# A fused Mamba and mixture-of-experts layer on one core: the load of C's row moves behind a slot's other loads, and the scaling of b2 moves four slots later

## The chip, the core and the metric

The kernel runs on one core of a Trainium2 chip. Time is the device time of one execution in microseconds (us), the median of several runs. The profile shows five engines: PE (TensorE), DVE (VectorE), ACT (ScalarE), POOL (GpSimd) and SP (SyncE, which here issues nearly all loads and stores and computes nothing). Each engine works through its own program in order and waits on semaphores for the others.

## The reference, cut to what matters

The input x is 4 x 2048 tokens of 512 features. The layer does two things to it.

```
mod = silu(c) @ wmod                       # six rows of 512 per batch: sa, ca, ga, sb, cb, gb
h = layernorm(x) * (1 + ca) + sa
x = x + ga * mamba(h)                      # ga, gb kept at least 0.25 from zero
h = layernorm(x) * (1 + cb) + sb
x = x + gb * moe(h)

mamba(h):  val, gate = split(h @ W_in);  val = silu(conv3(val))
           B, C = val @ W_B, val @ W_C;  delta = softplus((val @ W_delta + delta_base) @ W_tau)
           A_bar = exp(delta*A);  B_bar = expm1(delta*A)/(delta*A + 1e-6) * delta * B
           for each of 512 channels and 16 states:  s_t = A_bar_t * s_(t-1) + B_bar_t * val_t
           y_t = sum over the 16 states of s_t * C_t;  out = (y * silu(gate)) @ W_out + h
moe(h):    gates = top 2 of sigmoid(h @ gate_W), normalised
           sum over 8 experts of gate_e * (gelu(h @ W1_e + b1_e) @ W2_e + b2_e), plus one shared expert
```

## The kernel before, in words

The tokens are cut into 16 blocks of 512 (NQ). The recurrence is done in *units* of 128 channels by 1024 columns, 32 units in all. A unit has 16 states, and one state of one unit is one *slot* of the program: 512 slots, numbered c, behind 64 slots of lead-in (c below 0) and before 64 slots of tail. 32 slots make a *window*, r = c mod 32. In each slot every engine does its part of the recurrence for a state and, beside it, the steps of two other jobs that a table assigns to r: the *front* of a later block (normalise, the projections val, gate, B, C, delta, the convolution, all stored to DRAM) and the *FFN* of an earlier block (out projection, gating, the experts). PACE says how many steps of front and FFN go with a slot: one in the steady part, about 1.6 in slots 0 to 48, 1.5 in slots 448 to 512.

The recurrence of a slot goes over the engines like this:

- ACT makes `inv`, `th` and `abar` for four states at a time.
- PE broadcasts B's row to 128 partitions (L1162).
- DVE multiplies by u (L1179), by abar+1 (L1185), by the weight `inv` (L1191), by the ratio (L1198), and scans (L1209) into `hs`. These five are DVE's main work.
- POOL, in slot c: the product `hs * Cb` of state c-1 (`times_C`, L1363 or L1366), then steps of the FFN or front (newton L1397 to L1403, gating of the hidden rows L1452, and the split of B), then the weight `inv * th` of state c+2 (L1390), then it issues the accumulating DMA that adds `hs` of state c-1 to `ysum` (`add_to_y`, L1374 or L1377). That DMA waits until the one before it has landed (`y_summed`), because both add to the same tile. In this text y(c) is the transfer that adds state c's product.

`Cb` holds C's row of one state, broadcast to 128 partitions, in two buffers. SP loads the row of state c+1 in slot c (L680, 512 KB), after waiting for `hC_done >= c`, which is the product of state c-1, the last reader of that buffer. In the kernel before, this wait and load come first in SP's slot, and everything else that SP issues in the slot stands behind them:

```
for t in SLOTS:
    sync_slot(sp, t)                  # wait hC_done >= t; load Cb; then delta, us, Brow, gy and gated_y
    for H, r in steps_of(t):
        sync_steps(sp, H, r)          # loads and stores of the front and the FFN
    sync_slot_end(sp, t)              # the folding of ga and gb into W_out, W2 and b2
```

Many of the steps in `sync_steps` have waits of their own: a weight buffer (`aw`, `w1r`, `w2r`) is loaded when the matmuls that read it are done, a store waits for its producer. The steps named later: at r = 11 the loads of `gy` (L711) and of three `aw` (L535); at r = 13 the store of `gate_rows` (L567); at r = 23 a load of `w1r` (L544), a row of `gbc` (L564) and three `w2r` (L556); at r = 27 a load of `gy`; at r = 28 the loads of W_out into `w1r` (L654, 1 MB) and of the residual into `hf` (L656, 1 MB).

In slots -8 to 40 the kernel also folds ga and gb into the weights, one batch (12 slots) after another: SP loads a piece, POOL multiplies it (L1429), SP stores it. For b2 it is DVE that multiplies (L1217), into a piece of `w2r`, and SP stores the result (L739) at the end of slot 12b+5 for batch b. DVE may write the next batch's only when that store has landed (`fold_b2st`). In the kernel before DVE does this at the head of slots 12b-6, that is -6, 6, 18 and 30, each time (but the first) one slot behind the issue of the store it waits for.

Of the kernel before, what the change touches and what calls it, by code (L numbers as in the profile page):

```python
# [24 lines left out]
def adaln_mamba_moe(nc, x, W_val, W_gate, taps, W_BC, W_deltaT, delta_base, W_tau, A_log, W_out, gate_W, W1, b1, W2, b2,  # L25
# [7 lines left out]
    NB, L, D = x.shape  # L33
# [16 lines left out]
    WIN = 2 * N  # L50
# [27 lines left out]
    with ExitStack() as ctx:  # L78
# [8 lines left out]
        def ge(eng, s, value):  # L87
            if value > 0:
                eng.wait_ge(s, value)
# [329 lines left out]
        NF = 6  # L419
# [18 lines left out]
        def unit(c):  # L438
            return c // N
# [13 lines left out]
        def starts(u):  # L453
            return 0 <= u < NU and u in FIRST_U

        def fronts(u):
            q, n = BLOCKS[BLOCK_OF[u]]
            return q + n
# [209 lines left out]
            ge(sp, abar_done, N * (u - 1))  # L668
            sp.dma_start(tile_of(delta[:, u % 2, :], u), rows_of(delta_d, u)).then_inc(u_ld[u % 2], 16)

        def sync_slot(sp, c):
            r = c % WIN
            if 0 <= c + 1 < NC:
                u, n = unit(c + 1), (c + 1) % N
                q, size = BLOCKS[BLOCK_OF[u]]
                ge(sp, hC_done, c)
                if n == 0 and starts(u):
                    sp.wait_ge(st_c, 16 * fronts(u))
                row = c_d[q // 2, n, :] if size == 2 else c_d[q // 2, n, columns(q)]
                sp.dma_start(Cb[:, (c + 1) % 2, 0:size * T], row.partition_broadcast(P)).then_inc(C_ld[(c + 1) % 2], 16)  # L680
            if r in (1, 17) and 0 <= c // N + 1 < NU and not starts(c // N + 1):
                load_unit(sp, c // N + 1)
            if r in (8, 24) and 0 <= c // N + 1 < NU:
                u = c // N + 1
                if starts(u):
                    sp.wait_ge(st_u, 16 * fronts(u))
                ge(sp, uB_done, N * (u - 1))
                sp.dma_start(tile_of(us[:, u % 2, :], u), rows_of(u_d, u)).then_inc(us_ld[u % 2], 16)
            if r == 24 and starts(c // N + 1):
                k = BLOCK_OF[c // N + 1]  # L690
                q, n = BLOCKS[k]
                sp.wait_ge(st_b, 16 * (q + n))
                row = b_d[q // 2] if n == 2 else b_d[q // 2, :, :, columns(q)]
                if k > 1:
                    sp.wait_ge(B_ready, N * FIRST_U[k - 1])
                lo = BROW * (k % 2)
                sp.dma_start(Brow[lo:lo + 3 * N, 0:n * T], row.rearrange("j n t -> (j n) t")).then_inc(B_ld[k % 2], 16)
            if r in (2, 18) and 0 <= c // N - 1 < NU:
                u = c // N - 1
                sp.wait_ge(y_gated, u + 1)  # L700
                sp.dma_start(rows_of(gy_d, u), tile_of(gy[:], u)).then_inc(gy_st, 16)

            if r in (11, 27) and 0 <= c // N < NU:
                u = c // N
                ge(sp, gy_st, 16 * u)
                if u + 1 < NU:
                    sp.wait_ge(nr_minus, u + 2)
                    sp.wait_ge(nrd_done, u + 2)
                if starts(u):
                    sp.wait_ge(st_gate, 16 * fronts(u))  # L710
                sp.dma_start(tile_of(gy[:], u), rows_of(gate_d, u)).then_inc(gate_ld, 16)  # L711
# [456 lines left out]
        def dve_slot(dve, c):  # L1168
            v = nc.vector

            def X(c):
                return flat(ps[:, X_BANK + 2 * (c % 2):X_BANK + 2 * (c % 2) + 2, :])

            def times_u(c):
                if 0 <= c < NC:
                    u = unit(c)
                    dve.wait_ge(B_ready, c + 1)
                    dve.wait_ge(us_ld[u % 2], 16 * (u // 2 + 1))
                    v.scalar_tensor_tensor(X(c), X(c), 1.0, us[:, u % 2, :], ALU.mult, ALU.mult).then_inc(uB_done, 1)  # L1179

            def times_abar(c):
                if 0 <= c < NC:
                    dve.wait_ge(abar_done, c + 1)
                    dve.wait_ge(uB_done, c + 1)
                    v.scalar_tensor_tensor(X(c), abar[:, c % 4, :], 1.0, X(c), ALU.add, ALU.mult).then_inc(p1_done, 1)  # L1185

            def times_weight(c):
                if 0 <= c < NC:
                    dve.wait_ge(thinv_done, c + 1)
                    dve.wait_ge(p1_done, c + 1)  # L1190
                    v.scalar_tensor_tensor(X(c), X(c), 1.0, inv[:, c % 6, :], ALU.mult, ALU.mult).then_inc(pw_done, 1)  # L1191

            def times_ratio(c):
                if 0 <= c < NC:
                    u = unit(c)
                    dve.wait_ge(pw_done, c + 1)
                    for cols, g in parts(u):
                        ins = v.scalar_tensor_tensor(X(c)[:, cols], nrd[:, u % 2, cols], inv_kappa[:, c % N, g:g + 1],  # L1198
                                                     X(c)[:, cols], ALU.add, ALU.mult)
                    ins.then_inc(bu_done, 1)  # L1200

            def scan(c):
                if 0 <= c < NC:
                    u = unit(c)
                    dve.wait_ge(bu_done, c + 1)
                    if c >= 4:
                        dve.wait_ge(y_summed, 16 * (c - 3))
                    for cols, g in parts(u):
                        ins = v.tensor_tensor_scan(hs[:, c % 4, cols], abar[:, c % 4, cols], X(c)[:, cols],  # L1209
                                                   0.0 if begins(u) else carry[:, g, c % N:c % N + 1], ALU.mult, ALU.add)  # L1210
                    ins.then_inc(scan_done, 1)

            if 0 <= c + 6 < 2 * NF * NB and (c + 6) % (2 * NF) == 0:
                b = (c + 6) // (2 * NF)
                dve.wait_ge(fold_rows, 32 * (b + 1))
                ge(dve, fold_b2st, 16 * b)
                v.tensor_tensor(fold_b2g, b2g, gbc[BROW:BROW + EX, 1, :], ALU.mult).then_inc(fold_b2, 1)  # L1217
            times_weight(c)
            for H, r in steps_of(c)[:1]:
                dve_steps(dve, H, r, True)  # L1220
            times_ratio(c)
            times_u(c + 1)
            scan(c)
            times_abar(c + 1)
            for i, (H, r) in enumerate(steps_of(c)):
                if i:
                    dve_steps(dve, H, r, True)
                dve_steps(dve, H, r)
# [253 lines left out]
        with nc.Block() as block:  # L1482
            @block.sync
            def _(sp):
                for t in SLOTS:
                    sync_slot(sp, t)
                    for H, r in steps_of(t):
                        sync_steps(sp, H, r)
                    sync_slot_end(sp, t)
                for tt in range(TPB):  # L1490
                    sp.wait_ge(out_st[tt], 16 * NQ)
# [73 lines left out]
```

## Time and profile before

| | |
|---|---|
| median of 3 runs | 4697.77 us (4693.6 to 4699.59) |
| the profiled execution's own time | 4694.18 us |
| its span, first to last instruction | 4692.4 us |
| DVE busy | 4033.8 us (86%) |
| ACT busy | 3945.9 us (84%) |
| PE busy | 3849.1 us (82%) |
| POOL busy | 3647.7 us (78%) |
| granted TensorE clock, mean | 0.888 of full speed |
| moved by DMA | 1037.18 MB, mean 221 GB/s |

"Busy" is the sum of an engine's instruction times. No engine is at 100%, and the stretch matters: from 225 us to 774 us (slots 0 to 63) there is no FFN, from 774 us to 3860 us (slots 64 to 447) all three jobs run side by side, then the FFN is squeezed into fewer slots, and behind 4484 us (slot 511's scan) only the last FFN remains. A wait is listed under the engine that idled, with the line of the instruction it idled before, and behind the arrow what ended the wait.

### The profile page before, as it was taken

The numbers are of one execution on the slowest core, as the hardware profiler recorded it, in microseconds if no ns is written. First come the engines' busy times: TensorE is split into PE (matmuls) and PEld (weight loads), VectorE is DVE, ScalarE is ACT, GpSimd is POOL, SyncE is SP. The second block draws the span as 40 slices with busy tenths as digits, with TensorE's granted clock in tenths as the row PEclk, the third lists the DMA queues.
The fourth block names the chain that finished last, engine by engine and source line by source line (L and its number), as shares of the span: only waits on it lengthen the run. The fifth ranks groups of instructions, "written<-read, shape, count | busy, mean of one in ns | idle before, by whom it ended". The sixth has DMA issues, their size and how long they took to land.

```text
span 4692.4 us, 37024 instructions
## 1 busy us (share of the span) xinstructions
PE 3849.1 (82%) x9708; PEld 1612.3 (34%) x9708; DVE 4033.8 (86%) x3896; ACT 3945.9 (84%) x4282; POOL 3647.7 (78%) x2304
## 2 busy tenths in 40 slices
PE   6623413999899899989998998999998987988889
PEld 3201101333343333333343333333333333333344
DVE  1288899999999999999999999999999997887820
ACT  1698898998989898999989898989999897887811
POOL 0399987887889888888889888888888896767721
PEclk7856656999999999999999999999999988989889
DMA  3589867888888888888888888898988876657542
GB/s 131 197 247 266 236 170 198 238 235 255 231 253 233 257 246 258 232 251 248 242 255 234 254 235 258 236 267 221 264 252 236 238 210 166 192 154 196 138 146 67
DMA packets 352220, 1037.18 MB, mean 221 GB/s; under 512 B 41253, under 2 KB 44389, under 8 KB 344710
## 3 DMA queue, kind: packets, MB, share of 16 engines
q1 hardware_dynamic: 278282, 766.35, 47.9%
q0 software_dynamic: 73728, 268.47, 29.0%
q8 instruction: 78, 1.28, 0.1%
q14 instruction: 132, 1.08, 0.1%
HBM read 639.74 MB, written 126.51 MB: 163 GB/s over the span
## 4 chain that ended last, share of the span: by engine, by line
ACT 21%; PE 19%; DMA 13%; POOL 13%; issue 13%; DVE 8%; POOLq 0%; SPq 0%; DVEq 0%; ACTq 0%
DMA ysum<-hs 13%; PE ps L1125 7%; PE ps L1144 6%; POOL inv L1390 4%; POOL hs L1363 3%; ACT inv L761 3%; ACT th L772 3%; PE ps L1095 3%; ACT inv L767 3%; ACT abar L776 2%; ACT inv L754 2%; DVE ps L1191 2%; DVE ps L1179 2%; POOL ysum L1377 2%; DVE ps L1185 2%
## 5 line engine op out<-in xcount | busy, mean ns | idle before, releaser
L1390 POOL TENSOR_TENSOR inv<-inv,th 128x1024 f32<-128x1024 f32 x512 | 1268.0, 2477 | 148.8 <-ACT th L772 146.5
L1125 PE MATMUL ps<-hf,w1r 128*128 128x512 f32 x2304 | 1104.0, 632 | 38.6 <-ACT hid L884 23.3
L1363 POOL TENSOR_TENSOR hs<-hs,Cb 128x1024 f32<-128x1024 f32 x384 | 977.3, 2545 | 30.1 <-DVE hs L1209 13.2
L1162 PE MATMUL ps<-Brow,pick 48*128 48x512 bf16 x1024 | 346.6, 422 | 630.2 <-DVE hs L1209 629.1
L1144 PE MATMUL ps<-w2r,hid 128*128 128x512 f32 x1776 | 812.1, 604 | 0.8 <-ACT xn L884 0.7
L754 ACT ACTIVATE inv<-nrd,kappa 128x1024 f32<-128x1024 f32 (+1 forms) x640 | 578.6, 967 | 201.5 <-DVE ps L1191 197.4
L1179 DVE SCALAR_TENSOR_TENSOR ps<-ps,us 128x1024 f32<-128x1024 f32 x512 | 628.0, 1227 | 134.0 <-PE ps L1162 133.5
L1377 POOL DMA_DIRECT2D ysum<-hs x480 | 442.6, 922 | 367.4 <-DMA ysum<-hs 356.9
L1191 DVE SCALAR_TENSOR_TENSOR ps<-ps,inv 128x1024 f32<-128x1024 f32 x512 | 627.9, 1226 | 81.0 <-POOL inv L1390 59.2
L1198 DVE SCALAR_TENSOR_TENSOR ps<-nrd,inv_kappa,ps 128x1024 f32<-128x1024 f32 (+1 forms) x640 | 675.2, 1073 | 15.8
L1209 DVE TENSOR_TENSOR_SCAN hs<-abar,carry,ps 128x512 f32<-128x512 f32 (+1 forms) x384 | 683.5, 1801 | 0.3
L776 ACT ACTIVATE abar<-delta,negA 128x1024 f32<-128x1024 f32 (+1 forms) x640 | 605.6, 965 | 78.0 <-DVE hs L1209 78.0
L1125 PEld LDWEIGHTS ps<-hf,w1r 128*128 128x128 f32 x2304 | 448.7, 201 | 612.5 <-issue 562.9
L1185 DVE SCALAR_TENSOR_TENSOR ps<-abar,ps 128x1024 f32<-128x1024 f32 x512 | 618.2, 1207 | 0.1
L772 ACT ACTIVATE th<-delta,halfA 128x1024 f32<-128x1024 f32 (+1 forms) x640 | 605.2, 965 | 5.8 <-POOL inv L1390 5.8
L767 ACT ACTIVATE inv<-inv,ln_coef 128x1024 f32<-128x1024 f32 (+1 forms) x640 | 607.0, 967 | 1.5
L1209 DVE TENSOR_TENSOR_SCAN hs<-abar,ps 128x1024 f32<-128x1024 f32 (+1 forms) x256 | 511.6, 2009 | 0.3
L1144 PEld LDWEIGHTS ps<-w2r,hid 128*128 128x128 f32 x1776 | 332.1, 192 | 450.4 <-issue 447.5
L761 ACT ACTIVATE inv<-inv 128x2048 f32<-128x2048 f32 x256 | 478.9, 1902 | 1.3
L1162 PEld LDWEIGHTS ps<-Brow,pick 48*128 48x128 bf16 x1024 | 58.6, 97 | 991.1 <-DVE hs L1209 788.9
L1366 POOL TENSOR_TENSOR hs<-hs,Cb 128x1024 f32<-128x1024 f32 x128 | 311.7, 2435 | 35.6 <-DVE hs L1209 27.6
L1248 DVE TENSOR_TENSOR x<-ps,x 128x512 f32<-128x512 f32 x256 | 171.9, 682 | 170.4 <-PE ps L1144 147.6
(154 smaller groups left out, 5021.2 us busy)
## 6 DMA issues: line engine op xcount, KB each, us to landing
ysum<-hs POOLq DMA_DIRECT2D x512, 512.0 KB, 5.7
Cb<-c_rows SPq DMA_DIRECT2D x384, 512.0 KB, 4.6
w1r<-in_W SPq DMA_DIRECT2D x144, 512.0 KB, 5.3
w2r<-w_scaled SPq DMA_DIRECT2D x141, 512.0 KB, 8.1
Cb<-c_rows SPq DMA_DIRECT2D x128, 256.0 KB, 4.0
gbc<-expert_gates SPq DMA_DIRECT2D x128, 256.0 KB, 5.4
aw<-in_W_val SPq DMA_DIRECT2D x64, 256.0 KB, 6.3
xa<-in_x SPq DMA_DIRECT2D x32, 512.0 KB, 7.2
```

The source lines that it names most:

```text
L767: ins = s.activation(inv[:, c % 6, cols], inv[:, c % 6, cols], ACT.Exp, scale=-1.0, bias=ln_coef[:, c % N, g:g + 1])
L772: ins = s.activation(th[:, c % 3, cols], delta[:, u % 2, cols], ACT.Tanh, scale=halfA[:, c % N, g:g + 1])
L776: ins = s.activation(abar[:, c % 4, cols], delta[:, u % 2, cols], ACT.Exp, scale=negA[:, c % N, g:g + 1])
L1125: mm = t.matmul(o, w1r[:, n % 2, k, h * P:(h + 1) * P], hf[:, k, :], start=(k == 0), stop=(k == G - 1))
L1144: mm = t.matmul(o, hidden(e)[:, h, tt * P:(tt + 1) * P], (last_w2(e) if q == NQ - 1 and grp == 1 else w2r[:, e % 3])[:, h, :], start=(grp ...
L1179: v.scalar_tensor_tensor(X(c), X(c), 1.0, us[:, u % 2, :], ALU.mult, ALU.mult).then_inc(uB_done, 1)
L1185: v.scalar_tensor_tensor(X(c), abar[:, c % 4, :], 1.0, X(c), ALU.add, ALU.mult).then_inc(p1_done, 1)
L1191: v.scalar_tensor_tensor(X(c), X(c), 1.0, inv[:, c % 6, :], ALU.mult, ALU.mult).then_inc(pw_done, 1)
L1198: ins = v.scalar_tensor_tensor(X(c)[:, cols], nrd[:, u % 2, cols], inv_kappa[:, c % N, g:g + 1], X(c)[:, cols], ALU.add, ALU.mult)
L1209: ins = v.tensor_tensor_scan(hs[:, c % 4, cols], abar[:, c % 4, cols], X(c)[:, cols], 0.0 if begins(u) else carry[:, g, c % N:c % N + 1], ...
L1363: gp_.tensor_tensor(hs[:, c % 4, :], hs[:, c % 4, :], Cb[:, c % 2, :], ALU.mult).then_inc(hC_done, 1)
L1390: gp_.tensor_tensor(inv[:, c % 6, :], inv[:, c % 6, :], th[:, c % 3, :], ALU.mult).then_inc(thinv_done, 1)
```

## The change

SP's load of C's row is taken out of the head of `sync_slot` into a function `load_C` of its own, which is called after the front's and FFN's steps of the slot and before `sync_slot_end`. Its wait (`hC_done >= c`) goes with it. So what stood behind that wait in slot t now stands behind the wait of slot t-1 only, and the load of C's row stands behind whatever waits the slot's other steps have. DVE's scaling of b2 goes from slots 12b-6 to slots 12b-2 (-2, 10, 22, 34).

```
-        def sync_slot(sp, c):
-            r = c % WIN
+        def load_C(sp, c):
             if 0 <= c + 1 < NC:
                 u, n = unit(c + 1), (c + 1) % N
                 q, size = BLOCKS[BLOCK_OF[u]]
                 ...
                 row = c_d[q // 2, n, :] if size == 2 else c_d[q // 2, n, columns(q)]
                 sp.dma_start(Cb[:, (c + 1) % 2, 0:size * T], row.partition_broadcast(P)).then_inc(C_ld[(c + 1) % 2], 16)
+
+        def sync_slot(sp, c):
+            r = c % WIN
             if r in (1, 17) and 0 <= c // N + 1 < NU and not starts(c // N + 1):
...
-            if 0 <= c + 6 < 2 * NF * NB and (c + 6) % (2 * NF) == 0:
-                b = (c + 6) // (2 * NF)
+            if 0 <= c + 2 < 2 * NF * NB and (c + 2) % (2 * NF) == 0:
+                b = (c + 2) // (2 * NF)
                 dve.wait_ge(fold_rows, 32 * (b + 1))
                 ge(dve, fold_b2st, 16 * b)
...
                     for H, r in steps_of(t):
                         sync_steps(sp, H, r)
+                    load_C(sp, t)
                     sync_slot_end(sp, t)
```

## Rows read from the trace of the kernel before

**Rows 1.** The page's chain that ended last: shares of the span by line.
```profile
DMA ysum<-hs 13%; PE ps L1125 7%; PE ps L1144 6%; POOL inv L1390 4%; POOL hs L1363 3%; ACT inv L761 3%; ACT th L772 3%; PE ps L1095 3%; ACT inv L767 3%; ACT abar L776 2%; ACT inv L754 2%; DVE ps L1191 2%; DVE ps L1179 2%; POOL ysum L1377 2%; DVE ps L1185 2%
```

**Rows 2.** By stage: stretch, length, busy us PE, PEld, DVE, ACT, POOL; clock, DMA, GB/s.
```profile
225.00:656.00 431.00, 153.61 (x337) 52.85 (x338) 373.89 (x391) 373.19 (x515) 389.36 (x254) 0.63 0.82 239
774.00:3860.00 3086.00, 2783.76 (x7059) 1153.90 (x7057) 2974.82 (x2679) 2850.18 (x2799) 2648.88 (x1663) 0.94 0.85 244
```

**Rows 3.** Waits of DVE, 774 to 3860 us: total us, times, longest.
```profile
DVE ps L1191 <- POOL inv L1390: 54.1, 34, 3.6
```

**Rows 4.** Waits of POOL, 774 to 3860 us.
```profile
POOL ysum L1377 <- DMA ysum<-hs: 315.0, 120, 6.1
```

**Rows 5.** Waits, 3860 to 4484 us: DVE's largest.
```profile
DVE ps L1179 <- PE ps L1162: 102.5, 31, 7.6
```

**Rows 6.** Waits of DVE, 225 to 656 us.
```profile
DVE w2r L1217 <- DMA b_scaled<-w2r: 37.7, 3, 14.0
DVE ps L1191 <- POOL inv L1390: 4.4, 2, 3.2
```

**Rows 7.** POOL in time order behind DVE's three stalls: start, us, what, [idle <- releaser].
```profile
283.11 0.19 POOL L1359 COPY carry<-hs 128x2 f32<-128x2 f32 x1 [1.27 <-DVE hs L1209]
393.20 0.19 POOL L1359 COPY carry<-hs 128x2 f32<-128x2 f32 x1 [2.46 <-DVE hs L1209]
504.53 0.19 POOL L1359 COPY carry<-hs 128x2 f32<-128x2 f32 x1 [1.35 <-DVE hs L1209]
```

**Rows 8.** SP in order of time, r = 27 and 28 of one window.
```profile
2028.13 0.32 SPq L711 DMA_DIRECT2D gy<-gate_rows  x1
2033.99 0.48 SPq L654 DMA_DIRECT2D w1r<-w_out_scaled  x1
2034.52 0.52 SPq L656 DMA_DIRECT2D hf<-h_residual  x1
```

**Rows 9.** POOL in order of time there: y(26), y(27), y(28) are issued.
```profile
2029.48 1.73 POOL L1377 DMA_DIRECT2D ysum<-hs  x1
2035.75 1.00 POOL L1377 DMA_DIRECT2D ysum<-hs  x1
2047.31 0.88 POOL L1377 DMA_DIRECT2D ysum<-hs  x1 [3.55 <-DMA ysum<-hs]
```

**Rows 10.** The chain of waits in order of time: start, us, what.
```profile
1004.25 11.90 DMA ysum<-hs
...
2035.75 11.02 DMA ysum<-hs
...
3833.32 10.68 DMA ysum<-hs
```

**Rows 11.** SP, then POOL, in order of time around r = 11 of the next window.
```profile
2144.01 9.37 SPq L680 DMA_DIRECT2D Cb<-c_rows  x2
2153.49 0.39 SPq L711 DMA_DIRECT2D gy<-gate_rows  x1
2153.92 1.46 SPq L535 DMA_DIRECT2D aw<-in_W_val  x3
2168.25 0.46 SPq L567 DMA_DIRECT2D gate_rows<-xa  x1
...
2164.59 0.87 POOL L1377 DMA_DIRECT2D ysum<-hs  x1 [3.74 <-DMA ysum<-hs]
```

**Rows 12.** SP in order of time, r = 22 to 24, then POOL's product of state r = 24.
```profile
1992.73 0.32 SPq L680 DMA_DIRECT2D Cb<-c_rows  x1
1997.58 1.39 SPq L556 DMA_DIRECT2D w2r<-w_scaled  x3
...
2008.66 2.65 POOL L1363 TENSOR_TENSOR hs<-hs,Cb 128x1024 f32<-128x1024 f32 x1
```

**Rows 13.** The page's DMA issues (tile, KB each, median us to landing); below it Cb's spread.
```profile
ysum<-hs POOLq DMA_DIRECT2D x512, 512.0 KB, 5.7
...
DMA to landing us min/median/max: 3.0/4.5/12.9
```

More of the change, by code:

```diff
@@ L669, in load_unit, with load_C @@
             sp.dma_start(tile_of(delta[:, u % 2, :], u), rows_of(delta_d, u)).then_inc(u_ld[u % 2], 16)
-        def sync_slot(sp, c):
-            r = c % WIN
+        def load_C(sp, c):
             if 0 <= c + 1 < NC:
@@ L680, in sync_slot @@
                 sp.dma_start(Cb[:, (c + 1) % 2, 0:size * T], row.partition_broadcast(P)).then_inc(C_ld[(c + 1) % 2], 16)
+        def sync_slot(sp, c):
+            r = c % WIN
             if r in (1, 17) and 0 <= c // N + 1 < NU and not starts(c // N + 1):
@@ L1211, in scan @@
                     ins.then_inc(scan_done, 1)
-            if 0 <= c + 6 < 2 * NF * NB and (c + 6) % (2 * NF) == 0:
-                b = (c + 6) // (2 * NF)
+            if 0 <= c + 2 < 2 * NF * NB and (c + 2) % (2 * NF) == 0:
+                b = (c + 2) // (2 * NF)
                 dve.wait_ge(fold_rows, 32 * (b + 1))
@@ L1488, in _ @@
                         sync_steps(sp, H, r)
+                    load_C(sp, t)
                     sync_slot_end(sp, t)
```

## The prediction

> **What bounds the kernel now.** I read the busy times by stage first, then each engine's waits in the long stage, then the chain of waits, and last the order of time around the places that the change touches.
>
> The long stage, slots 64 to 447, takes 3086 us or 12 windows of 257 us, and DVE is busy in 2974.8 of them, 96% [rows 2]. The reader is to see two things there: DVE sets the pace, and it is idle for only 111 us. 54.1 us of that idle is in front of L1191, waiting for POOL's weight `inv` [rows 3], so 4.5 us a window is all that a faster POOL could give back. A slower POOL has no such limit. POOL itself waits 315.0 us for the previous accumulating transfer y [rows 4], 26 us a window, and these transfers are the largest line of the chain, 13% of the span [rows 1]. So POOL with its chain of y transfers runs level with DVE and overtakes it only at a few slots. What reaches POOL is how long each y takes: the median is 5.7 us [rows 13], and y(27), issued just behind two loads of 1 MB, takes 11.02 us and makes POOL wait 3.55 us before y(28) [rows 8, 9]. Eleven such y(27), from 1004.25 to 3833.32, stand in the chain of waits [rows 10].
>
> From 3860 to 4484 us PE decides: DVE waits 102.5 us for B's broadcast, its largest wait there [rows 5]. Behind 4484 us no row of C is loaded any more, and nothing changes. From 225 to 656 us (slots 0 to 48) DVE, ACT and POOL are busy 374, 373 and 389 of 431 us [rows 2]: nearly balanced, POOL a little ahead.
>
> **b2, four slots later.** Removed: DVE's three waits for the b2 store, 37.7 us [rows 6]. The scaling itself stays. Its store was issued at the end of slot 12b+5, the new place is five slots later instead of one, so the wait is gone and not moved. What is late next is POOL. Behind each of the three stalls POOL waited for DVE's scan by 1.27, 2.46 and 1.35 us [rows 7], together 5.1 us; its remaining time was work and transfers, which do not start earlier because DVE is free. The bounds are thus 5.1 and 37.7 us gained. DVE waited for POOL's weight by only 4.4 us in the whole stretch [rows 6], so behind the last stall it can run some way ahead of POOL's lead before it is caught. I take twice POOL's share: -10 us. From 656 us to 774 us there is no folding left for POOL, and the lead is kept.
>
> **What SP issues a slot earlier.** A step without a late wait of its own used to start when the product of state c-1 was done. Now it starts one product earlier, behind the previous row of C. No engine waits much for these loads, so their being early is worth nothing in itself. What changes is which y they run beside. Bytes and issues are the same; only the collisions move.
>
> At r = 28 SP issues W_out and the residual, 2 MB, at 2033.99, 1.8 us ahead of y(27) at 2035.75 [rows 8, 9]. They have been allowed for long, so after the change they follow at once on what r = 27 ends with. That is the load of `gy`, bound by its own wait at 2028.13, then C's row, then these two: about 2028.8 and 2029.3, just ahead of y(26) at 2029.48. I give y(26) the 11.02 us that y(27) has now; with `gy` and C's row beside it that is no overestimate. POOL can then issue y(27) at 2029.48 + 11.0 + 0.5 = 2041.0, not at 2035.75. Before, POOL had 2047.31 - 3.55 - 2035.75 = 8.0 us of work from y(27) to y(28), so y(28) comes at 2049.0, not 2047.31: 1.7 us late. The weights that POOL makes on the way come up to 5 us late, and DVE meets them where it has no slack, since this is the stretch where its waits for POOL lie. I take 2.0 us a window, 12 windows: +24 us. Bounds: 0 (y(27)'s gain pays for y(26)'s loss) and 5.2 us a window (2041.0 - 2035.75 with nothing recovered), +62 us.
>
> At r = 11 it goes the other way. The loads of `gy` and three `aw` (1.25 MB) stand at 2153.5 to 2155.4, around y(10), and POOL waits 3.74 us before y(11) [rows 11]. They move to the previous C load, 2144.4, and lie in the gap between two y. So this wait nearly goes. But the store of `gate_rows` (1 MB, 2168.25) also moves up by a slot, into y(11), and takes some back. Bounds 0 and 3.74 us a window; I take 1.0, since what POOL gains here must survive to the slots where DVE waits: -12 us.
>
> **The row of C behind the other steps.** A row of 512 KB lands in 4.5 us in the middle, 12.9 us at worst [rows 13], and mostly has a slot to spare. The worst place is r = 23: the row for the product at 2008.66 was issued at 1992.73 [rows 12]. Now it stands behind the `w1r`, `gbc` and three `w2r` loads, 2.25 MB, whose last waits end about 1997.6, and goes out at 1999.0. That leaves 9.7 us, between the middle and the worst landing. Late by 0 to 3 us a window; I take 0.5, so +6 us (bounds 0 and +36). In the stage after 3860 us SP waits longer for `w1r`, but PE decides there: 0.
>
> The Trainium skill (DMA: Bandwidth & Descriptors, Queues, rings and completion order) says that on each DMA engine the descriptors of one ring are consumed in ring order. By that rule C's row can't pass the loads ahead of it; its 12.9 us at worst agrees, and the sum above is by it.
>
> **The sum.** -10 + 24 - 12 + 6 = +8 us on the profiled execution's own 4694.18 us (span 4692.4 and 1.8 around it): 4702. The median of the runs shown is 3.6 us higher, 4697.77, so the forecast for a median is 4706 us. About 0.2% or 9.4 us is what a measurement of this kernel can tell from no change, so this is no change, on its slow side. The likeliest case's own range is 4695 to 4715.
>
> **The rivals.**
>
> *Slower: the collision at y(26) is paid in full.* Place: r = 28 of each window. Price: 5.2 us a window less DVE's present wait there. With 4.5 us of wait a window for POOL in all, I leave at most 1.5 to absorb it: 3.7 x 12 = 44 us, so 4706 - 24 + 44 = 4726. It decides from the point where POOL's delay exceeds what DVE has in hand at r = 31, 0 and 1. For it: eleven of the y(27) are in the chain [rows 10], so these slots are tight. Against it: y(27) itself becomes short, and y(28)'s wait of 3.55 us goes.
>
> *Faster: the loads no longer hit a transfer that counts.* If y(26) is little hurt by loads issued a bare microsecond ahead, the term of 24 us goes, y(28)'s wait goes with it (up to 3.55 us a window, of which DVE can use what it waits for POOL there, I take 1.0, 12 us), and the slot-11 gain and b2's stay: 4706 - 24 - 12 - 6 = 4664 with C's row in time. Against it: y(27) in its 11.02 us has 2.5 MB of loads issued ahead of it within 2.1 us; y(26) will have 3 MB within 1.4 us. Half way, 4682, is more likely than the end.
> The Trainium skill (DMA: Bandwidth & Descriptors, the same section) has each DMA engine go round-robin between the queue rows that have work, a packet at a time. By that rule the accumulating transfer on POOL's row would get half of each engine whatever SP has queued, and the move would cost nothing, as in this rival; the measured 11.02 us against a median of 5.7 speaks against an equal share, so the rule does not carry the sum.
>
> *b2's stall was on the path in full.* Then its term is -37.7, not -10, and the time is 4678. For it: DVE has hardly any other idle time there, 4.4 us for POOL. Against it: POOL's 389 us of work are more than DVE's 374 [rows 2], and the POOL waits that the stalls made are small [rows 7].
>
> *The change doesn't do what it says:* the steps of r = 28 or 11 have waits that hold them where they are. Then only b2 is left, 4688 to 4693. Against it: at 2033.99 they follow C's load at once.
>
> **How the numbers follow.** No change as summed: 0.36. Slower by y(26), with or without C's rows late: 0.33. Faster, through the transfers (0.14), b2 in full (0.12), or the change half empty (0.05): 0.31. The range leaves 0.1 at each side: its low end, 4663, is the faster transfers with all of their gain or b2 and some of them together, its high end, 4738, the slower rival with C's rows 1 us late in each window (+12). Faster by over 0.2%: 0.31, within 0.36, slower 0.33.
>
> **What would show it.** In the trace after: no wait in front of L1217 in DVE's list (before 37.7), and POOL's waits for DVE in 225 to 656 us smaller by some 5 us. Slots 0 to 48 shorter by about 10 us; by over 25, b2's rival is right. In each window y(26) about 11 us long and y(27) about 5, a wait of POOL before y(27) where there was none and none before y(28); if y(26) stays near 5 us, the term of 24 us is wrong. The wait before y(11) down from 3.7 us to 2 or less. DVE's wait for POOL's weight up from 54.1 us to some 70; if it falls below 40, the balance of the collisions was misjudged. POOL products that wait for C's row at r = 24, by at most 3 us: if others do, or if they wait longer, the cost of the new order was underrated. A stage from 3860 to 4484 us that changes by more than 5 us would be a mistake of its own, since I give it nothing.

## The result

| | before | after |
|---|---|---|
| median | 4695.69 us, 4 runs | 4797.09 us, 4 runs (4793.45 to 4799.68) |
| span of the profiled execution | 4692.4 us | 4797.9 us |

The ratio is 1.0216, 95% interval [1.0201, 1.0231]: 101 us slower. I had forecast 4706, called it no change, and given a range up to 4738: the sign of the sum was right, its size wrong by far, and the outcome that I held likeliest did not come.

Busy times hardly moved (DVE 4038.5 us, before 4033.8; POOL 3646.0, before 3647.7), so no work was added: the kernel waits more. From the page of the kernel after, the chain that ended last by line, two groups of instructions (busy, mean ns | idle before, releaser), and the transfers (KB each, median us to landing):

```profile
DMA ysum<-hs 13%; PE ps L1127 9%; PE ps L1146 8%; POOL hs L1365 3%; DMA Cb<-c_rows 3%; DVE ps L1181 3%; POOL inv L1392 3%; PE ps L1097 2%; DVE ps L1187 2%; DVE ps L1193 2%; ACT inv L763 2%; DVE hs L1211 2%; ACT th L774 1%; POOL ysum L1379 1%; ACT abar L778 1%
...
L1365 POOL TENSOR_TENSOR hs<-hs,Cb 128x1024 f32<-128x1024 f32 x384 | 969.2, 2524 | 98.9 <-DMA Cb<-c_rows 65.2
...
L1193 DVE SCALAR_TENSOR_TENSOR ps<-ps,inv 128x1024 f32<-128x1024 f32 x512 | 627.7, 1226 | 194.9 <-POOL inv L1392 175.5
...
ysum<-hs POOLq DMA_DIRECT2D x512, 512.0 KB, 5.6
Cb<-c_rows SPq DMA_DIRECT2D x384, 512.0 KB, 6.0
```

The reader is to see a line in the chain that [rows 1] does not have, C's row with 3%, and a product that waits for it. The median y did not get longer (5.6 us against 5.7 in [rows 13]). The averages say nothing here; what counts is which y is long. (Lines of after stand two below those of before: L1193 is the old L1191, L1365 the old L1363, L1379 the old L1377.)

A slot's length is told here from the end of one scan to the end of the next. Slots 64 to 447 took 3081.8 us before and 3180.8 after, +98.9; the part behind them +7.7; the part before them -1.1. So nearly the whole loss stands in the twelve windows, 8.2 us in each. The waits of DVE and POOL there, after (us in total, times, longest), to be held against [rows 3, 4]:

```profile
POOL ysum L1379 <- DMA ysum<-hs: 293.3, 114, 7.1
DVE ps L1193 <- POOL inv L1392: 146.6, 62, 6.1
POOL hs L1365 <- DMA Cb<-c_rows: 65.2, 21, 8.2
...
POOL ysum L1379 <- DMA Cb<-c_rows: 29.1, 13, 4.1
POOL carry L1361 <- DMA Cb<-c_rows: 29.0, 15, 5.4
```

DVE's wait for POOL's weight rose by 92.5 us (54.1 to 146.6), which is the loss but for 6 us. Waits for C's row are new. The 65.2 and 29.0 us before products are that. The 29.1 us put down to C's row before the issue of a y are not: the row landed within 0.5 us of the previous y, and each of these 13 issues came 0.5 to 0.9 us behind the landing of the previous y, which is what it waits for. So POOL's wait for y is 293.3 + 29.1 = 322.4 us, 7 more than before, and 94 us are for C's row. They are not at r = 24 alone: 31 us stand before the product of state r = 24, 32 before that of r = 6 and 17 before that of r = 20. The prediction had named this as the sign that the new order's cost was underrated. Which of these waits come out at DVE is for the experiments to tell.

One window in order of time. SP first (the y and products of POOL are in the next fence):

```profile
2027.10 0.33 SPq L544 DMA_DIRECT2D w1r<-in_W  x1
2027.47 0.46 SPq L564 DMA_DIRECT2D gbc<-expert_gates  x1
2027.97 2.79 SPq L556 DMA_DIRECT2D w2r<-w_scaled  x3
2030.80 0.59 SPq L679 DMA_DIRECT2D Cb<-c_rows  x1
...
2062.12 0.32 SPq L713 DMA_DIRECT2D gy<-gate_rows  x1
2062.49 0.43 SPq L679 DMA_DIRECT2D Cb<-c_rows  x1
2062.96 0.43 SPq L654 DMA_DIRECT2D w1r<-w_out_scaled  x1
2063.44 0.43 SPq L656 DMA_DIRECT2D hf<-h_residual  x1
```

```profile
2042.99 2.35 POOL L1365 TENSOR_TENSOR hs<-hs,Cb 128x1024 f32<-128x1024 f32 x1 [8.02 <-DMA Cb<-c_rows]
...
2063.78 1.43 POOL L1379 DMA_DIRECT2D ysum<-hs  x1
...
2075.85 0.88 POOL L1379 DMA_DIRECT2D ysum<-hs  x1 [5.94 <-DMA ysum<-hs]
...
2083.42 1.17 POOL L1379 DMA_DIRECT2D ysum<-hs  x1
...
2094.26 0.88 POOL L1379 DMA_DIRECT2D ysum<-hs  x1 [2.70 <-DMA ysum<-hs]
```

At r = 23 the row of C is issued at 2030.80 and the product gets it at 2042.99, 12.2 us later; POOL stands still for 8.02 us. This is one of the two longest of these waits in the twelve windows; their mean is 2.6 us. At r = 28 the 2 MB go out at 2062.96 and 2063.44, just ahead of y(26) at 2063.78, as predicted. What I had not followed is the next one: the loads of r = 30 (three `w2r`, 1.5 MB) also come a slot earlier, onto y(28). The chain of waits has both, y(26) with 11.53 us and y(28) with 10.31.

Before there was one long y in these slots, y(27), and a wait of 3.55 us [rows 9]; now there are two with one short y between them, and waits of 5.94 and 2.70 us.

### The profile page after: what moved, and what is told of

The parts are those of the page before. It is cut to its first block, busy times and chain, and to the rows that moved or that the text cites. A ratio compares the mean times of both kernels' runs of the same rounds, so it can differ in the third digit from the quotient of the medians.

```text
span 4797.9 us, 37024 instructions
## 1 busy us (share of the span) xinstructions
PE 3883.9 (81%) x9708; PEld 1637.2 (34%) x9708; DVE 4038.5 (84%) x3896; ACT 3948.8 (82%) x4282; POOL 3646.0 (76%) x2304
## 4 chain that ended last, share of the span: by engine, by line
PE 23%; DMA 17%; issue 14%; POOL 12%; DVE 12%; ACT 11%; SPq 1%; POOLq 0%; DVEq 0%; ACTq 0%
DMA ysum<-hs 13%; PE ps L1127 9%; PE ps L1146 8%; POOL hs L1365 3%; DMA Cb<-c_rows 3%; DVE ps L1181 3%; POOL inv L1392 3%; PE ps L1097 2%; DVE ps L1187 2%; DVE ps L1193 2%; ACT inv L763 2%; DVE hs L1211 2%; ACT th L774 1%; POOL ysum L1379 1%; ACT abar L778 1%
## 5 line engine op out<-in xcount | busy, mean ns | idle before, releaser
L1365 POOL TENSOR_TENSOR hs<-hs,Cb 128x1024 f32<-128x1024 f32 x384 | 969.2, 2524 | 98.9 <-DMA Cb<-c_rows 65.2
L1146 PE MATMUL ps<-w2r,hid 128*128 128x512 f32 x1776 | 831.7, 616 | 0.1
L1193 DVE SCALAR_TENSOR_TENSOR ps<-ps,inv 128x1024 f32<-128x1024 f32 x512 | 627.7, 1226 | 194.9 <-POOL inv L1392 175.5
L1379 POOL DMA_DIRECT2D ysum<-hs x480 | 442.7, 922 | 379.2 <-DMA ysum<-hs 343.0
```

What stands on the lines that cost most here:

```text
L1146: mm = t.matmul(o, hidden(e)[:, h, tt * P:(tt + 1) * P], (last_w2(e) if q == NQ - 1 and grp == 1 else w2r[:, e % 3])[:, h, :], start=(grp ...
L1365: gp_.tensor_tensor(hs[:, c % 4, :], hs[:, c % 4, :], Cb[:, c % 2, :], ALU.mult).then_inc(hC_done, 1)
```

## The experiments

In all of them the b2 move of the change is in, except where said. All keep every instruction and byte; they change only where SP's program has the load of C's row, or one other load. Each ratio is against runs of the kernel before that were made beside it, with medians from 4695.01 to 4697.02 us; a step of a few us between two medians is not told from none. In the diffs `C_first` is a condition: where it holds, `load_C` stands at the head of slot t as before, otherwise behind the steps as in the change. "b2 alone" below is the first kernel.

**b2 alone, and the order alone.**

```
  kernel 1: DVE's b2 scaling at 12b-2; SP's order as before
  kernel 2: DVE's b2 scaling at 12b-6 as before; SP's order as changed
```

> The kernel before with b2's scaling four slots later and nothing else. Theory A (b2's stall is covered in part by POOL, in part by PE's own wait for aw at the same place): 0 to -12 us on 4696, ratio 0.9975 to 1.000, the wait in front of b2's scaling gone, and in its place, at slot 19, a wait of DVE for PE's broadcast of B of several us. Rival B (the stall was on the path in full): -30 to -38 us, ratio 0.992 to 0.9935. Rival C (the late scaling itself costs something, and is part of the loss of 101 us): slower by 10 us or more.

Measured: 4689.22, ratio 0.9991 [0.998, 1.0001], as Theory A had it.

> The order of SP alone: the load of C's row behind the slot's other steps, b2's scaling at its old place. Theory A (the order is the whole loss): +100 to +112 us, ratio 1.021 to 1.024. Rival (the two parts need each other, since without the b2 stall the front runs into SP's queue): +70 us or less, ratio under 1.015.

Measured: 4800.07, ratio 1.0214 [1.019, 1.0237]. The order is the whole loss, and b2 a gain of about 4 us (6 by the medians) that can't be told from none.

Where b2's 37.7 us went is in the waits of the b2-alone kernel, 225 to 656 us, against [rows 6]:

```profile
DVE hT L1254 <- PE ps L1081: 19.3, 4, 10.8
...
PE ps L1081 <- DMA aw<-w_delta_tau: 17.2, 2, 9.1
DVE ps L1191 <- POOL inv L1390: 16.2, 13, 2.9
DVE ps L1179 <- PE ps L1162: 16.1, 2, 12.7
```

The wait before L1217 is gone. DVE is 18 us ahead of the kernel before at the start of slot 32 and 3.8 us at slot 48. POOL's weight takes 16.2 - 4.4 = 12 us back, where the prediction had left 27.7 to it; PE takes more. In the kernel before, the two waits of DVE for PE in this fence came to 6.9 and 2.4 us, now to 19.3 and 16.1, together 26 us more, and PE's wait for `aw` (w_delta_tau) to 8.7, now 17.2. The loads of `aw` stand behind other waits of SP's program; the b2 stalls had been lying over that.

**The wait kept at the head of the slot, only the load moved behind.**

```
                 for t in SLOTS:
+                    if 0 <= t + 1 < NC:
+                        ge(sp, hC_done, t)
                     sync_slot(sp, t)
                     ...
+                    load_C(sp, t)
```

> The kernel after, but SP waits for the product (hC_done) at the head of the slot again and only then issues the slot's other steps, with the load of C's row behind them. So nothing is issued earlier than in the kernel before, and C's rows are as late as in the kernel after or later. Theory A (two costs: loads issued a slot earlier run into transfers y that count, some 60 to 75 us, and C's row late at r = 24, some 25 us): +15 to +40 us on 4696, ratio 1.003 to 1.0085; y(26) back at 5 us, y(27) at 11, POOL's product at r = 24 still waits 2 to 3 us. Rival B (C's row behind the others is the whole loss): +90 us or more, ratio above 1.019. Rival C (the early loads are the whole loss): within 0.3% of the kernel before.

Measured: 4707.24, ratio 1.0027 [1.0017, 1.0037], 18 us above b2 alone, a little under Theory A's lower end. So the late rows alone cost 18, three times my 6; the rest of the loss needs the steps a slot earlier. The place is the one that the prediction named: by the mean over the twelve windows slot 27, a few slots behind the late product of r = 24, takes 11.0 us against 8.6 with b2 alone. That is 28 us, and later slots give some of it back. POOL's waits for C's row at other slots do not show at DVE in this way.

**Single slots put back into the old order.**

```
-                    load_C(sp, t)          # behind the steps, all slots
+                    C_first = t % WIN == 28        # then: == 23; then: in (23, 28, 30)
```

> The kernel after, with C's load at the head again in one slot of 32, r = 28, so that the 2 MB of W_out and residual wait for the product as in the kernel before. Theory A (their early issue beside y(26) makes POOL's wait of 6 us before y(27), and from it the 4.2 us longer slot 31): 45 to 55 us of the 101 come back, ratio 1.010 to 1.013, y(26) 5 us and slot 31 under 9 us. Rival B (another transfer takes its place, y(27) or y(28) beside the early w2r loads of r = 30): less than 20 us come back, ratio above 1.017.

Measured: 4733.07, ratio 1.0084 [1.0064, 1.0103]. 64 us come back from one slot in 32, more than Theory A had. In this kernel y(28) is shorter too, 7.5 us in the mean against 10.0, and the wait before y(29) goes from 2.4 to 0.2, although r = 30 is left in the new order. So the 64 us hold part of what r = 30 costs.

> The kernel after, with C's load at the head again only in the slots r = 23, so that the row for r = 24 does not stand behind w1r, gbc and three w2r loads. Theory A (that row's lateness, 2.6 us of POOL's waiting a window, is what makes slot 27 longer by 2.0 us): 20 to 30 us of the 101 come back, ratio 1.0155 to 1.0175, POOL's wait at r = 24 gone, slot 27 back to 9 us, slot 31 as in the kernel after (12 us). Rival B (POOL's wait is absorbed by the waits for transfers behind it, and slot 27 stays): under 8 us come back, ratio above 1.020.

Measured: 4774.22, ratio 1.0167 [1.0147, 1.0186]: 23 us, Theory A.

> The kernel after, with C's load at the head again in three slots of 32: r = 23, 28 and 30 (30 holds back gbc and three w2r, which run into y(28)). Theory A (these three places are the whole loss): ratio 0.998 to 1.003, slots 27, 31, 0 and 1 together within 1 us of the kernel before. Rival B (the other slots whose steps are early or whose rows of C are late cost as well, as slot 14, which is 0.8 us longer): ratio 1.004 to 1.008.

Measured: 4746.33, ratio 1.0106 [1.0089, 1.0124]. Both theories missed: three slots put back give less than r = 28 alone. The trace shows a new collision that this mixture of orders makes. SP, then POOL:

```profile
2060.96 1.55 SPq L556 DMA_DIRECT2D w2r<-w_scaled  x3
2062.56 0.58 SPq L664 DMA_DIRECT2D h_residual<-hT  x1
...
2075.59 0.88 POOL L1379 DMA_DIRECT2D ysum<-hs  x1 [3.06 <-DMA ysum<-hs]
```

With r = 30 held back and r = 31 not, the three `w2r` and the store of the residual, 2.5 MB, go out together and just ahead of y(29), which is issued at 2064.36. But this is not where the 19 us over the next kernel stand: slots 31, 0 and 1 together are no longer than there. Slot 27 is 1.4 us longer (y(22) takes 10.3 us, there 8.9) and slot 4 is 0.9 us longer, while slot 14 is 1.0 us shorter. Why y(22) is longer stays open; for slot 4 see the kernel with the new order in slots 2 to 21.

```
+                    C_first = t % WIN in (23, 28)
```

> The changed kernel with the row of C first again in slots r = 23 and r = 28 alone (r = 30 stays in the new order). Theory A, the places are additive: putting r = 28 back returned 64 us and r = 23 returned 23 us, so together 87, about 4710 us (ratio to before 1.003). Theory B, what a place costs depends on where the loads of the neighbouring slots stand: then r = 23, 28 and 30 together gave less than r = 28 alone (4746 against 4733), and this kernel too comes out above 4725. Under A slot 27 is back at 9.0 us and slot 31 at 7.6.

Measured: 4727.63, ratio 1.0063 [1.0048, 1.0079]. Theory B held: once r = 28 is put back, r = 23 is worth 5 us by the medians, which overlapping intervals don't tell from none, and not 23. Places do not add up in the total. At the place itself they do: with C's row late at r = 23, slot 27 is 2.2 to 2.4 us longer in each of four pairs of kernels (27 to 29 us in twelve windows): three that differ in this slot alone, and the one with the wait kept at the head against b2 alone. What changes is how much the slots behind it, 28 to 1, give back.

**The new order outside the windows' end.**

```
+                    C_first = t % WIN not in range(2, 22)
```

> The changed kernel with the new order only in slots r = 2 to 21; r = 22 to 31, 0 and 1 have the row of C first as before. Theory A (all the loss sits at r = 23 and 28 to 30): within 0.2% of before, 4689 to 4700. Theory B (some 10 to 20 us sit elsewhere, such as slot 14's +0.8 us a window and waits for C's row at r = 6, 17 and 20): 4703 to 4715.

Measured: 4714.45, ratio 1.0035 [1.0024, 1.0046]: 25 us above b2 alone. In this stretch, where I had counted a gain of 12, the order loses. The loss comes in single events and not in each window: five of the slots 14 are 1.6 to 3.3 us longer than before, slot 356 is 5.2 us longer and slot 471 5.4. POOL's products and copies wait 43 us for C's row in the long stage, yet DVE's wait for its weight is only 5 us longer than with b2 alone (60.4 against 55.2). DVE's wait for PE's broadcast grows by 10 (25.1 to 34.8), and PE's wait for rows `xn` that POOL makes is new (0.9 to 30.3):

```profile
DVE ps L1181 <- PE ps L1164: 34.8, 25, 4.1
PE ps L1106 <- POOL xn L1446: 30.3, 10, 4.7
```

The slots 14 go with the granted clock of TensorE. Here are a stretch that ends in a slot 14 of 7.2 us and one that ends in one of 11.3 (stretch, length, busy us PE, PEld, DVE, ACT, POOL; clock, DMA, GB/s):

```profile
3201.50:3212.70 11.20, 10.56 (x29) 4.58 (x28) 11.06 (x9) 11.12 (x10) 6.50 (x5) 0.85 0.49 130
3458.20:3473.60 15.40, 15.40 (x42) 8.86 (x41) 11.12 (x9) 15.30 (x14) 11.62 (x10) 0.65 0.75 196
```

In the second the clock is at its lower level, 1.2 GHz (0.50), from 3455.2 to 3468.9, after PE had stood idle for 4.68 us waiting for `xn` and 2.35 us waiting for a scan; the router's 32 matmuls (L1112) take 7.0 us there and 3.7 in the first, and DVE waits 4.14 us for B's broadcast. So a likely path is: C's row late, POOL late with `xn`, PE idle, clock down, broadcast late. In the long stage PE's wait for `xn` is 12.5 to 36.7 us in the kernels with C's row behind the steps in slots 2 to 21, and at most 2.8 in all the others. But no run takes this path alone, and slots 14 of 9.7 us occur in the others too.

At slot 356 an instruction of DVE takes 5.35 us whose median over its 16 cases is 167 ns. Two of POOL's run beside it. The fence has it and the second of these (start, us, what):

```profile
3120.15 5.35 DVE L1316 TENSOR_TENSOR uu<-uu,vhalo 128x8 f32<-128x8 f32 x1
3122.83 2.63 POOL L1392 TENSOR_TENSOR inv<-inv,th 128x1024 f32<-128x1024 f32 x1
```

It ends 0.04 us behind POOL's. All 42 cases of this instruction over 0.9 us, in all the traces, end 0.03 to 0.04 us behind an instruction of POOL's. So this small addition of DVE can be held up by POOL, by 5 us here, and whether it meets POOL is a matter of a fraction of a us. In the kernel with three slots put back nine windows have it, with 1.0 to 3.4 us each, and that is what makes its slot 4 longer. In the residual kernel below one case takes 5.16.

**The new order at r = 11 alone.**

```
+                    C_first = t % WIN != 11
```

> b2 four slots later, C's load at the head everywhere but in the slots r = 11, where it stands behind the loads of gy and three aw: only these are issued a slot earlier. Theory A (what POOL gains before y(11), 3.7 us a window, reaches the slots 27, 0 and 1): 8 to 20 us faster than with b2 alone (0.9991), ratio 0.995 to 0.9975. Rival B (POOL meets DVE's scan between r = 11 and 13, so nothing reaches slot 27): the wait before y(11) goes all the same, and the ratio stays 0.9985 to 1.0.

Measured: 4693.77, ratio 0.9994 [0.9985, 1.0003], no gain over b2 alone. The wait before y(11) is gone, in every window. But POOL, 4 us earlier, now stops where it had not stopped. In the window below it does so at the next two products, because DVE has not scanned yet:

```profile
2159.51 2.35 POOL L1365 TENSOR_TENSOR hs<-hs,Cb 128x1024 f32<-128x1024 f32 x1 [1.45 <-DVE hs L1211]
...
2166.68 2.35 POOL L1365 TENSOR_TENSOR hs<-hs,Cb 128x1024 f32<-128x1024 f32 x1 [1.70 <-DVE hs L1211]
```

Over the whole long stage POOL waits 43 us less for y than with b2 alone (310.1 to 267.3), and more for DVE's scan (12.9 to 26.8), for ACT's `th` (56.1 to 70.7) and for ACT's `bc_sb` (4.9 to 22.4). DVE's wait for POOL's weight does not move.

**Building the loss up, slot by slot.** From b2 alone, C's row goes behind the steps at r = 28; at 28 and 30; at 23, 28 and 30.

```
+                    C_first = t % WIN != 28        # then: not in (28, 30); then: not in (23, 28, 30)
```

> One part alone: the order of before (and b2 four slots later), with C's row behind the other steps at r = 28 only. Theory A (W_out's and the residual's 2 MB just ahead of y(26) is the main loss and stands by itself): about 60 us slower than the b2-only kernel, 4745 to 4755, slot 31 some 3.5 to 4 us longer, y(26) at 11 us. My prediction's own price was 24 us, 4713. Theory B (it needs the early w2r loads of r = 30 behind y(28) as well): 4710 to 4730, since y(28) stays below 6 us here.

> The order of before (b2 four slots later), with C's row last at r = 28 and r = 30. r = 28 alone cost 26 us against b2 alone (4715 against 4689); r = 2 to 21 alone cost 25. Theory A, the two collisions one behind the other (y(26), then y(28) beside the early w2r loads of r = 30) leave POOL no slot to catch up: 45 to 60 us slower than b2 alone, 4734 to 4749, slot 31 near 11.9 us. Theory B, r = 30 is worth nothing by itself: 4712 to 4720, slot 31 at 10.8 as in the r = 28 kernel.

> As before this one, with r = 23 as a third slot in which C's row is last. In the changed kernel r = 23 was worth 23 us while r = 28 was late, and only 5 once r = 28 was put back (4733 to 4728). Theory A (places weigh more together, because POOL meets y(26) without its lead): 15 to 25 us above the kernel with r = 28 and 30 alone, 4755 to 4770, and with the 25 us of r = 2 to 21 this makes the changed kernel's 4797 nearly whole. Theory B: 5 us above.

Measured, with DVE's wait for POOL's weight in slots 64 to 447 of each trace beside it:

| C's row behind the steps at | median us | ratio to before | step | DVE's wait |
|---|---|---|---|---|
| nowhere (b2 alone) | 4689.22 | 0.9991 [0.998, 1.0001] | | 55.2 |
| 28 | 4714.96 | 1.0035 [1.0023, 1.0047] | +26 | 77.3 |
| 28, 30 | 4734.89 | 1.0085 [1.0057, 1.0113] | +20 | 101.0 |
| 23, 28, 30 | 4773.59 | 1.0166 [1.0145, 1.0187] | +39 | 139.4 |
| everywhere (the change) | 4797.09 | 1.0216 [1.0201, 1.0231] | +24 | 146.6 |

The first step is Theory B's, the second Theory A's; the third ends 4 us above Theory A's range. The rows behind the last column, from the waits of the kernel with 28:

```profile
DVE ps L1193 <- POOL inv L1392: 77.3, 51, 4.7
```

of the kernel with 28 and 30:

```profile
DVE ps L1193 <- POOL inv L1392: 101.0, 55, 4.7
```

and of the kernel with 23, 28 and 30:

```profile
DVE ps L1193 <- POOL inv L1392: 139.4, 57, 5.7
```

Each step of time has its step in this one wait, to within 5 us, up to the last. That one stands elsewhere: of the +24 (26.6 between the two profiled executions), slot 14 has about 14 us, by DVE's wait for PE's broadcast (18.9 to 29.4 in the long stage), slot 31 has 4, and 9 stand behind slot 447. The new order in slots 2 to 21 has the same two signs, the slots 14 and slot 471, by itself. In the kernel with r = 28 alone the picture in order of time is the predicted one. SP:

```profile
2033.01 0.43 SPq L654 DMA_DIRECT2D w1r<-w_out_scaled  x1
2033.49 0.43 SPq L656 DMA_DIRECT2D hf<-h_residual  x1
```

and POOL's y(26), y(27), y(28):

```profile
2034.55 1.18 POOL L1379 DMA_DIRECT2D ysum<-hs  x1
2045.87 0.88 POOL L1379 DMA_DIRECT2D ysum<-hs  x1 [5.45 <-DMA ysum<-hs]
2053.41 1.17 POOL L1379 DMA_DIRECT2D ysum<-hs  x1
```

By the mean over the twelve windows, slot 31 grows by 3.0 us against b2 alone (7.8 to 10.8) and slot 0 gives 1.0 back (8.9 to 7.9): 2.0 us a window, the prediction's own number. With r = 30 as well, y(28) takes 9.8 us in the same window, POOL waits 2.17 us before y(29), and slot 1 grows by 1.8 us (9.2 to 11.0). POOL there, y(28) and y(29):

```profile
2066.04 1.17 POOL L1379 DMA_DIRECT2D ysum<-hs  x1
2076.39 0.88 POOL L1379 DMA_DIRECT2D ysum<-hs  x1 [2.17 <-DMA ysum<-hs]
```

With r = 23 slot 27 grows by 2.4 us (8.6 to 11.0) and slots 31 and 1 by 0.4 to 0.5 more. In its window POOL comes to the product of r = 24 behind a y that was itself waited for:

```profile
2035.55 0.88 POOL L1379 DMA_DIRECT2D ysum<-hs  x1 [2.67 <-DMA ysum<-hs]
2038.63 2.35 POOL L1365 TENSOR_TENSOR hs<-hs,Cb 128x1024 f32<-128x1024 f32 x1 [2.21 <-DMA Cb<-c_rows]
```

**The other way: fewer bytes beside one y.** The order of before, but the load of the residual (1 MB) goes from r = 28 to r = 29, so that the two loads of 1 MB are a slot apart.

```
             if r == 28:
                 if has(qx):
                     ...
                     sp.dma_start(wout, woutg_d[qx // QPB]).then_inc(wo_ld, 16)
+            if r == 29:
+                if has(qx):
                     sp.wait_ge(st_h, 16 * (qx + 1))
                     sp.dma_start(hf[:], h_d[qx]).then_inc(h_ld, 16)
```

> b2 four slots later, SP's order as before, and the residual's load (1 MB) moved from r = 28 to r = 29, so that y(27) and y(28) have 1 MB beside them each instead of y(27) 2 MB. Theory A (a transfer y costs only what it takes beyond POOL's 8 us of work to the next one): y(27) about 7.5 us, y(28) about 7, no wait before y(28), DVE's waits for POOL at slots 0 and 1 (2.2 us a window) mostly gone: 12 to 30 us faster, ratio 0.9935 to 0.9975. Rival B (the 1 MB then runs into y(28) and y(29) with the w2r loads of r = 30, which only moves the wait by a slot): ratio 0.998 to 1.002.

Measured: 4674.70, ratio 0.9957 [0.9943, 0.997]: 20 us faster than before, 15 below b2 alone. y(27) takes 8.1 us in the mean (10.9 before), the wait before y(28) falls from 3.3 to 0.5, and slot 0 from 9.1 to 7.5. DVE's wait for the weight in slots 64 to 447, against [rows 3]:

```profile
DVE ps L1195 <- POOL inv L1394: 29.3, 20, 3.6
```

**And the `aw` loads of the first slots ahead of other waits.** This kernel has the residual's load at r = 29 too; the edit shown comes on top of that.

```
+                    early = 0 <= t < 2 * WIN
+                    if not early:
+                        load_C(sp, t)
+                        sync_slot(sp, t)
                     for H, r in steps_of(t):
                         sync_steps(sp, H, r)
+                    if early:
+                        load_C(sp, t)
+                        sync_slot(sp, t)
```

> The kernel with the residual's load at r = 29 (4674.7), and in slots 0 to 63 SP does the front's steps first, then C's row and the stores and loads of the recurrence, so that the loads of aw (w_delta_tau) no longer stand behind the store of gated_y and C's wait. If PE's wait of 9 us for aw at slot 19 (and a like one at slot 40) is what eats b2's 18 us, some 5 to 12 us more come back: 4663 to 4670. If the aw buffers are not free any earlier, or C's row behind the steps is late, no gain: 4672 to 4680.

Measured: 4670.39, ratio 0.994 [0.9925, 0.9954]. This is the fastest of all, but its interval overlaps that of the kernel without the edit, so the edit's own gain is not shown. PE still waits for `aw` there, a little less than the 16.3 us (longest 9.2) without the edit:

```profile
PE ps L1085 <- DMA aw<-w_delta_tau: 11.6, 2, 6.6
```

## Why the prediction was wrong

- **What bounds the kernel: right.** POOL runs level with DVE, slowing it has no limit and speeding it has one. The ladder shows the first, the r = 11 kernel the second.
- **b2, -10 us:** right in kind, measured -6 by the medians and -4 by the ratio, neither told from nothing. "What is late next is POOL" named the smaller part of what was late next: POOL's weight took 12 us back, PE 26. That the size came near was partly luck.
- **r = 28 onto y(26), +24 us: right.** Alone it costs 26, with y(26) at 10.8 us in the mean, 5.45 us of wait before y(27) and none before y(28) in its window. The rival that had it "paid in full" at 44 was too dear; this slot does absorb half.
- **"What changes is which y they run beside": applied to two slots only. This is the step that failed first.** I looked at r = 28 and r = 11 and not at r = 30, although a step's move must be followed for every load it issues. The three `w2r` onto y(28) cost 20 us, once y(26) was late, that no term of the sum had.
- **r = 11, -12 us: wrong, 0.** The collision went as foreseen; but the wait it made was not on the path: what POOL gains there is stopped by DVE's scan and by ACT in the slots behind it. For slots 2 to 21 I had a gain of 12 and the new order has a loss of 25.
- **C's row behind r = 23's loads, +6 us: the largest error of size, and the step that cost most.** The sum took 9.7 us from issue to use and thought 0.5 us late. The row took 11.1 us to land in the mean of the windows and 12.2 to its use in the one shown, where its wait was 8.02 us; the product waits 2.6 us in the mean. Price: 18 us for all late rows without the earlier steps, 39 us for r = 23 on top of 28 and 30, 5 us (not told from none) with r = 28 put back. That it is the late row, and not r = 23's own steps a slot earlier, is shown by slot 27, which is 2.3 us longer in the kernel without earlier steps and 2.4 in the ladder. The upper bound I had given, 36, was for a row 3 us late; I should have gone by the worst landing of [rows 13], 12.9 us, since the row stood behind 2.25 MB.
- **The sum itself.** I added the terms as if each found POOL in the same state. A delay at one place costs the same there, but the slots behind it give some back if they have slack and nothing if the next delay stands in them. r = 28 is worth 26 us alone and 64 within the change, r = 23 is worth 5 or 39.
- **Behind 3860 us, 0: wrong by 7.7 us,** 6.0 of it at one slot (471). POOL waits for C's row in that stage too, 10.0 us at the longest, and from slot 464 to 470 its products start 9 to 14 us behind the scans, where they started 4 to 8 behind:

```profile
POOL carry L1361 <- DMA Cb<-c_rows: 28.9, 5, 10.0
```

Added up, the error of 93 us (101 measured against a sum of +8) is: r = 30, 20; r = 23, 39 - 6 = 33; the other slots, 24 + 12 = 36; b2, 4 to 6; r = 28, 2. That is 95 to 97; the medians agree no better than that. Of the 24 in the other slots, 14 stand at slot 14 and 9 behind slot 447, and which row or step makes them was not taken alone. The shares hold for this order of adding the places; in another order they would differ.

## What to carry to other kernels

Where an in-order queue of loads is reordered, list every load that moves and the transfer it now runs beside, not only the largest. Price the result on the path of the resource that runs level with the bound: a delay there is paid, a gain is stopped at the next wait on another engine, and a delay with another one behind it has no slack to be made up in. When a few bytes must be waited for soon, count what stands ahead of them in their queue. The best lever found was the opposite of a reorder: keeping two loads of 1 MB a slot apart.

## What the runs showed of the hardware

The accumulating transfer of 512 KB has a wide spread that goes by what SP has issued just ahead of it. In the kernel after:

```profile
DMA to landing us min/median/max: 4.3/5.7/12.7
```

It took 11.53 us behind 3 MB issued in the 2 us ahead (2062.12 to 2063.87), 10.31 behind the loads of r = 30, and about 4.6 when next to nothing went out around it. In the residual kernel, with 1 MB ahead and 1 MB a few us later, y(27) took 8.1 us in the mean.

The packets tell where the time goes. The accumulating transfers are queue q0, SP's are q1 (packets, MB, share of the 16 DMA engines' time). First the y of 11.53 us, issued at 2063.78: from there to 2069.3, then from 2069.3 to 2075.0; last the short y(27) issued at 2075.85, from 2077.3 to 2080.1:

```profile
q1 hardware_dynamic: 360, 1.75, 92.9%
...
q1 hardware_dynamic: 190, 1.30, 57.2%
q0 software_dynamic: 144, 0.52, 46.1%
...
q0 software_dynamic: 143, 0.52, 98.9%
```

The short one has its first packet 1.4 us after its issue and moves everything in 2.8 us. The long one has its first packet only after 5.6 us, in which the engines move SP's bytes alone, and then needs another 5.6 us, twice 2.8, beside SP's. So about 4 us of the delay come before its first packet and 3 us from sharing. The y(27) of the kernel before are alike, with the first packet 4.9 us after the issue in the mean. Why the first packet comes late, no run here tells.

The Trainium skill (DMA: Bandwidth & Descriptors, Queues, rings and completion order) lets each DMA engine take turns between the queue rows that have work, a packet at a time. The trace agrees for the time in which both queues have packets under way: q0 has 46.1% of the engines there. The prediction read 11.02 us against a median of 5.7 as speaking against an equal share; the time that an equal share doesn't account for stands before the first packet. It was right not to let the rule carry the sum.

C's row, 512 KB as well, lands in 3.6 to 3.7 us in the mean of the windows where nothing stands ahead of it (r = 23 and 27 before); behind 2.25 MB it took 11.1 us in the mean of the windows after, and over all rows the worst went from 12.9 [rows 13] to 14.7:

```profile
DMA to landing us min/median/max: 3.0/5.5/14.7
```

The Trainium skill, in the same section, has one ring's descriptors consumed in order, and here the trace agrees.
